# TensorE's units beside attention cut into parts of at most four products, shared results kept in a place of their own, the feed-forward's first stages eight slots earlier

## The chip, the core and the metric

The program runs on one core of one Trainium2 chip. A core has five engines with a queue each: TensorE (PE, matrix products into PSUM banks), VectorE (DVE), ScalarE (ACT), GpSimd (POOL) and SyncE (SP, which only issues DMAs here). The metric is the device time of one execution in microseconds (us), the median over several runs.

## What is computed

One layer: an attention of an unusual kind, then a feed-forward part with routed experts, each between layer norms and with a residual. The input x is 4 batches of 2048 rows of 256 numbers, all in fp32. The reference, cut to what matters:

```python
# attention: per head one scalar z for each key and query row
Z = concat([k @ Wproj.T, q @ Wproj.T], axis=1)
# out_i = sum_j max(0, 1 - |z_i - z_j| / b_h) * v_j   (the reference sorts and sums prefixes)
ctx = ctx / T
x = x + layernorm(attention(layernorm(x)))
# feed-forward on h = layernorm(x), 8192 rows
gu = h @ shared_gate_up_w                       # 256 -> 2 x 512
shared = silu(gu[:, :512]) * gu[:, 512:] @ shared_down_w
shared = shared * sigmoid(h @ shared_gate_w)
w, idx = top_k(softmax(h @ gate_w), 8)          # 64 experts, capacity 128 each
y = routed experts on the gathered rows, weighted and added
x = x + layernorm(y + shared)
```

## The kernel before

**The attention loop.** The kernel doesn't sort. For each of the 4 batches b it goes through 256 slots (`SLOTS`), 1024 tiles in all. A tile is the 128x2048 matrix of weights of 128 keys of one head against all 2048 queries. In slot n, ScalarE writes |z_query - z_key| for a tile (line 1085), VectorE turns it into min(., 1) - 1 in place (line 1406), and TensorE multiplies it with V in `tensor_step` (line 886): four matmul calls of 128x32 by 512 columns, on four groups of array columns side by side. Step n takes quarter c of tile n - c, so that a tile is fully used three steps after its own. The tiles lie in a ring of 8 (`NTB`), and ScalarE waits with tile n until tile n - 8 is used (`tile_used`), which means until TensorE has begun step n - 5. 64 slots (a quad) finish four heads. In the first slots of the next quad TensorE transposes their results (`tensor_quad_out`, line 847) and VectorE copies them (lines 1323 and 1331).

**Own tiles.** ScalarE needs longer for a tile than VectorE, so VectorE makes some tiles alone (lines 1428 and 1404). `own_tiles` picks them: it adds up, slot by slot, what VectorE has left after the work beside attention, with the costs in `WEIGHTS`, and gives it a tile when it is far enough ahead. It picks 86 tiles, 19, 23, 22 and 22 in the four batches.

**The work beside attention.** All else that the loop carries is written in `timetable(b)`: one list of (slot, unit) for each of TensorE, VectorE, ScalarE and SyncE. Each engine's program goes through the slots in order and, ahead of the tile of slot n, does the entries that are due. The lists fix only the order on each engine. When an entry really runs is set by semaphores. In batch 0 the loop carries the front of batches 1 to 3 (f): for each chunk k of 512 rows load, norm, transposes (`xT`), values (`v`), then the sixteen steps `z` that build z for the batch, with weights that SyncE loads into a ring of three buffers (`ml`). In batches 1 to 3 it carries the rest of batch b - 1: the residual and its norm (rows, `rows_at`), then from `rest_at(k)`, for each chunk k: norm (`hn`), transposes (`hT`), router logits (`lg`), routing on VectorE and GpSimd (`rm`, `re`, `sc`, `sm`), the transposed mask (`mT`), the shared gate and up products (`gu`: 4 pieces m, each one unit for gate and one for up), and the shared down products (`dn`), whose results go to y_rows in DRAM.

**Units on TensorE.** `tensor_stage` issues a whole unit at once, ahead of the step of its slot. A unit ends in one PSUM bank; banks 4, 5 and 6 are used in turn (`bank_uses`). In matmul calls: `gu` 2 of 512 columns, `z` 2 of 512 in each of 16 entries, `v` 4 of 256, `lg` 8 of 65 in two entries, `dn` 8 of 256, `hT`, `xT` and `mT` 4 transposes. The profile shows two MATMUL instructions for a call (line 828: 512 instructions for 256 calls), and one for a transpose.

**The place of the shared results.** `y_of(b, k)` shares its place in `scr` with `h_of(b, k)`. So `dn` on VectorE waits for the store of h, and `hn` of chunk k waits for the store of y of chunk k - 1 (line 1224).

**After the loop.** The last batch's rest runs in a tail: its routing, then 64 expert steps (`tensor_tail`), with the shared units of chunks 1 to 3, one in every second step (`shared_in_step`), and a last pass over all rows.

## Time and profile before

| | |
|---|---|
| median of 3 runs | 2416.1 us (2409.9 to 2416.64) |
| the profiled execution | 2415.98 us |
| its span, first to last instruction | 2414.7 us |
| VectorE, ScalarE, TensorE busy | 83%, 81%, 80% |
| mean granted clock of TensorE | 0.919 |
| ScalarE's first tile of the loop starts at | 80.18 us |
| the four batches of the loop begin on VectorE at | 83, 594, 1064 and 1536 us |
| the loop ends, the tail begins | 2003 us |
| expert steps, last pass | 2097 to 2330 us, 2330 us to the end |

An engine's busy share is a mean over stages with different limits. Within the loop three engines are busy most of the time and hand tiles on to each other, so what counts is which of them waits, and for whom.

### The profile page before, as it was taken

To read this page: it belongs to the slowest core of one execution; us is meant where nothing else is said; L and a number is where in the kernel's file an instruction comes from. 1 tells how busy PE (TensorE), PEld (TensorE's weight loads), DVE (VectorE), ACT (ScalarE), POOL (GpSimd) and SP (SyncE) were. 2 spreads that over 40 slices of the span, in tenths; PEclk is the share of its full clock that TensorE was granted. 3 is DMA by queue.
4 is the path that set the end of the run, shared out by engine and by line. 5 is a ranking of instruction groups with operands and counts; after the bars stand their busy time and mean duration, and the time that the engine had idled before them with its cause. 6 is when DMAs were issued, how large, how long until landed. Compare 5 with 4: busy or idle time off the path is not lost.

```text
span 2414.7 us, 30201 instructions
## 1 busy us (share of the span) xinstructions
PE 1930.5 (80%) x11666; PEld 760.1 (31%) x11666; DVE 1994.5 (83%) x2847; ACT 1948.2 (81%) x1290; POOL 1007.4 (42%) x372
## 2 busy tenths in 40 slices
PE   7689889789668889886798898777898896899920
PEld 4333233233112223221132232212223224677710
DVE  4598888887999998999998999998989897644348
ACT  2498998898999999999998999999999995122223
POOL 1010110100336367263383574550853764377754
PEclk9899999899889999998998999988999998898965
DMA  6326244335120212131202021312020306488779
GB/s 224 133 66 222 81 154 149 110 127 185 57 105 12 90 31 81 42 114 44 96 20 92 20 94 33 116 38 96 27 85 20 101 3 148 125 227 228 182 207 306
DMA packets 182037, 259.23 MB, mean 107 GB/s; under 512 B 22280, under 2 KB 162184, under 8 KB 173704
## 3 DMA queue, kind: packets, MB, share of 16 engines
q1 hardware_dynamic: 167408, 237.83, 29.3%
q0 software_dynamic: 12288, 18.88, 4.1%
q8 instruction: 93, 1.52, 0.3%
q10 hardware_dynamic: 2200, 0.60, 0.1%
q14 instruction: 48, 0.39, 0.0%
HBM read 187.25 MB, written 70.03 MB: 107 GB/s over the span
## 4 chain that ended last, share of the span: by engine, by line
PE 32%; DVE 26%; ACT 26%; POOL 6%; issue 5%; DMA 3%; SPq 0%; DVEq 0%; POOLq 0%; ACTq 0%
ACT TB L1085 25%; PE ps L886 12%; DVE TB L1406 10%; PE ps L790 5%; DVE TB L1428 4%; PE ps L828 4%; PE ps L835 3%; DVE st L1139 3%; DVE TB L1404 2%; PE ps L981 2%; POOL scr L1579 2%; POOL rs L1561 2%; POOL ve L1559 2%; DMA y_rows<-ZB 1%; PE ps L773 1%
## 5 line engine op out<-in xcount | busy, mean ns | idle before, releaser
L1085 ACT ACTIVATE TB<-ZB,nzk 128x2048 f32<-128x2048 f32 x938 | 1795.6, 1997 | 144.2 <-PE ps L886 98.0
L886 PE MATMUL ps<-TB,V 128*32 128x512 f32 x8192 | 1098.1, 636 | 282.5 <-DVE TB L1406 266.0
L1406 DVE TENSOR_SCALAR TB<-TB 128x2048 f32<-128x2048 f32 x938 | 1130.0, 1230 | 100.0 <-ACT TB L1085 97.9
L886 PEld LDWEIGHTS ps<-TB,V 128*32 128x32 f32 x8192 | 206.7, 112 | 1004.7 <-DVE TB L1406 630.7
L1579 POOL TENSOR_TENSOR scr<-ebase,scr 128x256 f32<-128x256 f32 x12 | 510.5, 42542 | 0.0
L1559 POOL TENSOR_SCALAR ve<-mv 128x4 f32<-128x4 f32 x56 | 82.5, 1472 | 800.4 <-DVE mv L1143 800.4
L828 PE MATMUL ps<-XF,wsgu 128*128 128x512 f32 x512 | 259.8, 632 | 1.2 <-DVE TB L1313 0.7
L1428 DVE SCALAR_TENSOR_TENSOR TB<-ZB,kz 128x2048 f32<-128x2048 f32 x86 | 212.4, 2469 | 4.2 <-PE ps L886 4.2
L1577 POOL TENSOR_TENSOR scr<-ebase,scr 128x4 f32<-128x4 f32 x12 | 28.5, 2378 | 390.0 <-DVE scr L1267 390.0
L1118 ACT ACTIVATE ZB<-ps 128x128 f32<-128x128 f32 x64 | 17.8, 278 | 184.0 <-PE ps L981 155.8
L828 PEld LDWEIGHTS ps<-XF,wsgu 128*128 128x128 f32 x512 | 91.8, 197 | 148.6 <-issue 141.6
L1404 DVE TENSOR_SCALAR TB<-TB,kz 128x2048 f32<-128x2048 f32 x86 | 121.6, 1414 | 0.0
L1684 POOL DMA_INDIRECT y_rows<-ZB x64 | 102.2, 1597 | 31.4 <-issue 14.9
L1561 POOL TENSOR_TENSOR rs<-ve,mhalf 128x4 f32<-128x4 f32 x56 | 106.1, 1894 | 4.7
L790 PE MATMUL ps<-scr,XF 128*128 128x512 f32 x192 | 100.1, 644 | 0.0
L835 PE MATMUL ps<-wsdn,XF 128*128 128x256 f32 x384 | 89.3, 386 | 0.0
L1670 POOL DMA_INDIRECT TB<-h_rows,ZB x64 | 63.5, 993 | 60.0 <-ACT ZB L1125 25.8
L1526 DVE COPY ZB<-ps 128x256 f32<-128x256 f32 x64 | 27.0, 422 | 67.0 <-PE ps L971 54.2
L835 PEld LDWEIGHTS ps<-wsdn,XF 128*128 128x128 f32 x384 | 71.0, 190 | 28.8 <-issue 20.1
L1610 POOL TENSOR_TENSOR scr<-scr,ctxn 128x1024 f32<-128x1024 f32 x12 | 61.0, 5080 | 36.0 <-DVE ctxn L1149 36.0
L847 PE MATMUL ps<-ident,cT 128*128 128x128 f32 x248 | 41.9, 295 | 39.3 <-DVE ctxn L1331 39.0
L1323 DVE COPY cT<-ps 128x512 f32<-128x512 f32 x60 | 41.3, 688 | 37.3 <-PE ps L886 37.2
(190 smaller groups left out, 1621.8 us busy)
## 6 DMA issues: line engine op xcount, KB each, us to landing
ZB<-zq_rows SPq DMA_DIRECT2D x64, 1024.0 KB, 7.0
scr<-fused_w SPq DMA_DIRECT2D x48, 512.0 KB, 3.5
TB<-in_egu_w SPq DMA_DIRECT2D x44, 256.0 KB
y_rows<-zero SPq DMA_DIRECT2D x20, 512.0 KB, 4.8
fused_w<-TB SPq DMA_DIRECT2D x4, 2048.0 KB, 13.7
TB<-y_rows SPq DMA_DIRECT2D x16, 512.0 KB, 8.5
XF<-in_x SPq DMA_DIRECT2D x24, 256.0 KB, 3.2
v_rows<-scr SPq DMA_DIRECT2D x24, 256.0 KB, 2.1
```

Source lines behind the costliest of these rows:

```text
L790: ins = pe.matmul(ps[bank][:, :], view(X0, NT * c + tt, [[16, 128]]), w[:, c, :], start=(tt == 0 and c == 0), stop=(tt == 15 and c == 1))
L828: ins = pe.matmul(ps[bank][:, :], wsgu[:, c, o:o + 128], hT_of(b, k)[:, c, :], start=(c == 0), stop=(c == 1))
L835: ins = pe.matmul(ps[bank][:, 256 * t:256 * t + 256], act_of(b)[:, mm, 128 * (2 * i + t):128 * (2 * i + t) + 128], wsdn[:, mm, :], start=( ...
L886: ins = pe.matmul(ps[c][32 * j:32 * j + 32, :], V[:, o:o + 32], tile(t)[:, 512 * c:512 * c + 512], start=(kb == 0), stop=(kb == KB - 1))
L1085: act.activation(tile(e), zrow(head), ACT.Abs, bias=nzk[b][:, kb * H + g:kb * H + g + 1], scale=1.0).then_inc(s_abs, 1)
L1404: dve.tensor_scalar(T, T, top, top, ALU.min, ALU.subtract).then_inc(s_bump, 1)
L1406: dve.tensor_scalar(T, T, 1.0, 1.0, ALU.min, ALU.subtract).then_inc(s_bump, 1)
L1428: dve.scalar_tensor_tensor(tile(e), zrow(head), kz[:, 0, kb * H + g:kb * H + g + 1], zrow(head), ALU.subtract, ALU.max, reverse0=True).the ...
L1559: pool.tensor_scalar(ve[s][:, :], view(mv[s][:, 0, 1:2], 0, [[2, 4]]), eps, None, ALU.add).then_inc(s_p, 1)
L1561: pool.tensor_tensor(rs[s][:, :], ve[s][:, :], mhalf[:, 0:4], ALU.pow).then_inc(done, 1)
L1579: pool.tensor_tensor(E4[:, :, 0:64], view(ebase[:, 0:1], 0, [[0, 4], [0, 64]]), E4[:, :, 0:64], ALU.pow).then_inc(s_ex, 1)
L1684: pool.indirect_dma_start(Y[c], bass.IndirectOffsetOnAxis(ap=idx2[:, order[n]:order[n] + 1].bitcast(u32), axis=0), ye[n % NX], None, compu ...
```

## The change

Every entry of TensorE's list is now a unit and a part of it (`PARTS`): `gu` in 2 parts of one matmul call, `z` in 32 of one call, `v` in 2 and `lg` in 4 parts of two calls. `dn` becomes 4 units of 128 rows in place of 2 of 256, each in 2 parts of two calls. The largest part is so four MATMUL instructions. The timetable gives each part a slot of its own: `gu` takes two slots of every three, `dn` the eight slots from r + 46 to r + 53, `z` eight slots of every nine, 36 in place of 32 for a batch. Rows stand 10 slots apart in place of 12 and begin one slot earlier, `rest_at` is 52 + 48k in place of 60 + 48k, the front's chunks stand 9 apart in place of 10. Within the rest most of VectorE's entries stand one to four slots later after `rest_at` than before.

In batches 0 to 2 the results of `dn` go to `wv_sb` and a free part of `scr` (`y_rows`), stored by two DMAs of 256 KB each in place of one of 512 KB. `dn` no longer waits for the store of h but for the store of the y before it, and `hn` of chunk k waits for the store of h of chunk k - 1 and for its transposes in place of the store of y. In the tail the 30 shared units become 36, spread over steps 1 to 59.

```diff
-           "rm": 15, "re": 8, "sc": 14, "sm": 5, "sg": 4, "gu": 7, "dn": 8}
+           "rm": 15, "re": 8, "sc": 14, "sm": 5, "sg": 4, "gu": 7, "dn": 4}
+
+PARTS = {"xT": 1, "hT": 1, "mT": 1, "zT": 1, "v": 2, "z": 32, "lg": 4, "gu": 2, "dn": 2}
...
-    return 8 + 12 * blk
+    return 7 + 10 * blk
...
-    return 60 + 48 * blk
+    return 52 + 48 * blk
...
-    return 2 + 86 * (f - 1) + 10 * blk
+    return 1 + 85 * (f - 1) + 9 * blk
...
-    return front_at(f, 3) + 20 + 2 * tt
+    return front_at(f, 3) + 21 + 9 * tt // 4
...
-            sy += [(r - 2, "xl", p, k), (r + 9, "h", p, k), (r + 31, "cum", p, k), (r + 58, "w2", p, k), (r + 50, "y", p, k)]
+            sy += [(r - 2, "xl", p, k), (r + 9, "h", p, k), (r + 33, "cum", p, k), (r + 58, "w2", p, k), (r + 58, "y", p, k)]
             dv += [(r, "xst", p, k, 0), (r + 1, "xst", p, k, 1), (r + 5, "hn", p, k, 0), (r + 6, "hn", p, k, 1),
-                   (r + 12, "hT", p, k), (r + 20, "lg", p, k), (r + 21, "rm", p, k), (r + 23, "re", p, k),
-                   (r + 28, "sc", p, k), (r + 40, "sg", p, k), (r + 54, "sm", p, k)]
+                   (r + 12, "hT", p, k), (r + 21, "lg", p, k), (r + 22, "rm", p, k), (r + 24, "re", p, k),
+                   (r + 31, "sc", p, k), (r + 41, "sg", p, k), (r + 55, "sm", p, k)]
             ac += [(r + 15, "hT", p, k)]
-            pe += [(r + 8, "hT", p, k, 0), (r + 9, "hT", p, k, 1), (r + 15, "lg", p, k, 0), (r + 16, "lg", p, k, 1),
-                   (r + 24, "mT", p, k)]
+            pe += [(r + 8, ("hT", p, k, 0)), (r + 9, ("hT", p, k, 1)), (r + 27, ("mT", p, k))]
+            pe += [(r + 15 + t, ("lg", p, k), t) for t in range(4)]
             for m in range(4):
-                for up in range(2):
-                    pe += [(r + 17 + 6 * m + 3 * up, "gu", p, k, m, up)]
-                ac += [(r + 23 + 6 * m, "gu", p, k, m)]
-                dv += [(r + 24 + 6 * m, "gu", p, k, m)]
-            for i in range(2):
-                pe += [(r + 42 + 3 * i, "dn", p, k, i)]
-                dv += [(r + 46 + 3 * i, "dn", p, k, i)]
+                g = r + 19 + 6 * m
+                pe += [(g + 3 * up + c, ("gu", p, k, m, up), c) for up in range(2) for c in range(2)]
+                ac += [(g + 7, "gu", p, k, m)]
+                dv += [(g + 7, "gu", p, k, m)]
+            for i in range(4):
+                pe += [(r + 46 + 2 * i + h, ("dn", p, k, i), h) for h in range(2)]
+                dv += [(r + 50 + 2 * i, "dn", p, k, i)]
...
-            dv += [(r - 1, "fst", f, k, 0), (r, "fst", f, k, 1), (r + 3, "fn", f, k, 0), (r + 4, "fn", f, k, 1), (r + 9, "xT", f, k, 0), (r + 9, "xT", f, k, 1)]
-            pe += [(r + 5, "xT", f, k, 0), (r + 6, "xT", f, k, 1)]
+            dv += [(r, "fst", f, k, 0), (r + 1, "fst", f, k, 1), (r + 5, "fn", f, k, 0), (r + 6, "fn", f, k, 1),
+                   (r + 12, "xT", f, k, 0), (r + 12, "xT", f, k, 1)]
+            pe += [(r + 8, ("xT", f, k, 0)), (r + 9, ("xT", f, k, 1))]
             for i in range(2):
-                pe += [(r + 10 + 2 * i, "v", f, k, i)]
-                dv += [(r + 14 + 2 * i, "v", f, k, i)]
-                sy += [(r + 15 + 2 * i, "vs", f, k, i)]
+                pe += [(r + 13 + 2 * i + t, ("v", f, k, i), t) for t in range(2)]
+                dv += [(r + 18 + 2 * i, "v", f, k, i)]
+                sy += [(r + 19 + 2 * i, "vs", f, k, i)]
         for tt in range(16):
-            pe += [(z_at(f, tt), "z", f, tt)]
+            pe += [(z_at(f, tt) + c, ("z", f), 2 * tt + c) for c in range(2)]
             sy += [(z_at(f, tt) - 5, "ml", f, tt)]
         r = z_at(f, 15)
-        dv += [(r + 6, "z", f), (r + 13, "zT", f)]
-        pe += [(r + 7, "zT", f)]
-        sy += [(r + 14, "zq", f)]
+        dv += [(r + 5, "z", f), (r + 10, "zT", f)]
+        pe += [(r + 6, ("zT", f))]
...
+        o += gate_units(b, k) + [("dn", b, k, i) for i in range(4)]
...
-    return o[n // 2:n // 2 + 1] if n >= 0 and n % 2 == 0 else []
+    return [u for i, u in enumerate(o) if 1 + 60 * i // len(o) == n]
...
+            if b == last:
+                return rows4(view(T0, 1024 * k, [[256, 4], [1, 256]]))
+            return [wv_sb[:, 0, :], wv_sb[:, 1, :], view(S0, 3652, [[1, 256]]), view(S0, 3908, [[1, 256]])]
...
+                    sp.wait_ge(q_h[3], 16 * b)
...
-                kk, m = use["dn", b, k, 1]
+                kk, m = use["dn", b, k, 3]
                 sp.wait_ge(empty[kk], m + 1)
-                sp.dma_start(Yv[0][4 * b + k], y_of(b, k)).then_inc(q_y, 16)
+                for i in range(2):
+                    src = view(y_rows(b, k)[2 * i], 0, [[256, 2], [1, 256]])
+                    sp.dma_start(Yv[0][4 * b + k][:, 2 * i:2 * i + 2, :], src).then_inc(q_y, 16)
...
+        def tensor_stage(unit, part=None):
+            for p in range(PARTS[unit[0]]) if part is None else (part,):
+                tensor_part(unit, p)
+
...
+            out_, ends = ps[bank], p == PARTS[what] - 1
+            if p == 0 and m:
...
+                if p == 0:
+                    for kk, mm in [use["xT", b, j, h] for j in range(4) for h in range(2)]:
...
+                if b and c == 0:
...
-                for c in range(2):
-                    ins = pe.matmul(ps[bank][:, :], view(X0, NT * c + tt, [[16, 128]]), w[:, c, :],
-                                    start=(tt == 0 and c == 0), stop=(tt == 15 and c == 1))
-                if tt == 15:
+                ins = pe.matmul(out_[:, :], view(X0, NT * c + tt, [[16, 128]]), w[:, c, :], start=(p == 0), stop=ends)
+                if ends:
                     ins.then_inc(full[bank], 1)
-                elif b:
+                elif b and c:
                     ins.then_inc(s_zm, 1)
...
+                if p == 0:
+                    for c in range(2):
+                        kk, mm = use["hT", b, k, c]
+                        pe.wait_ge(empty[kk], mm + 1)
+                o = NS * unit[4] + 128 * i
+                ins = pe.matmul(out_[:, :], wsgu[:, p, o:o + 128], hT_of(b, k)[:, p, :], start=(p == 0), stop=ends)
+                if ends:
+                    ins.then_inc(full[bank], 1)
...
+                if p == 0:
+                    kk, mm = use["gu", b, k, 3, 1]
...
+                for mm in (2 * p, 2 * p + 1):
+                    ins = pe.matmul(out_[:, 0:256], act_of(b)[:, mm, 128 * i:128 * i + 128], wsdn[:, mm, :],
+                                    start=(mm == 0), stop=(mm == 3))
+                if ends:
+                    ins.then_inc(full[bank], 1)
...
-                    dve.wait_ge(q_y, 16 * (4 * b + k))
+                    dve.wait_ge(q_h[k - 1], 16 * (b + 1))
+                    kk, mm = use["hT", b, k - 1, 1]
+                    dve.wait_ge(full[kk], mm + 1)
...
-                    dve.wait_ge(q_y, 192)
+                    dve.wait_ge(q_h[3], 16 * last)
...
-                    dve.wait_ge(q_h[k], 16 * (b + 1))
+                    dve.wait_ge(q_y, 32 * (4 * b + k))
...
-                for t in range(2):
-                    ti = 2 * i + t
-                    ins = dve.tensor_scalar(y_of(b, k)[:, ti, :], ps[bank][:, 256 * t:256 * t + 256],
-                                            sg[:, 4 * k + ti:4 * k + ti + 1], None, ALU.mult)
-                ins.then_inc(empty[bank], 1)
+                dve.tensor_scalar(y_rows(b, k)[i], ps[bank][:, 0:256], sg[:, 4 * k + i:4 * k + i + 1], None,
+                                  ALU.mult).then_inc(empty[bank], 1)
```

## Rows read from the trace of the kernel before

**Rows 1.** The page: granted clock by slices, the two costliest groups.

```profile
PEclk9899999899889999998998999988999998898965
...
L1085 ACT ACTIVATE TB<-ZB,nzk 128x2048 f32<-128x2048 f32 x938 | 1795.6, 1997 | 144.2 <-PE ps L886 98.0 <-DMA ZB<-zq_rows 45.8
...
L1406 DVE TENSOR_SCALAR TB<-TB 128x2048 f32<-128x2048 f32 x938 | 1130.0, 1230 | 100.0 <-ACT TB L1085 97.9
```

**Rows 2.** Busy time by windows, batches 0 and 2 (us, busy with instruction counts, clock).

```profile
83.00:594.00 511.00, 434.54 (x2570) 159.71 (x2570) 426.20 (x507) 460.58 (x240) 48.18 (x24) 0.93 0.40 139
...
1064.00:1536.00 472.00, 390.78 (x2480) 119.48 (x2480) 435.29 (x534) 453.96 (x255) 240.53 (x37) 0.94 0.19 66
```

**Rows 3.** ScalarE's tiles by lines: windows 83:594, 594:1064, 1064:1536, 1536:2003.

```profile
L1085 ACT ACTIVATE TB<-ZB,nzk 128x2048 f32<-128x2048 f32 x240 | 461.1, 1994 | 50.9 <-PE ps L886 45.9 <-DMA ZB<-zq_rows 4.8
...
L1085 ACT ACTIVATE TB<-ZB,nzk 128x2048 f32<-128x2048 f32 x232 | 444.0, 1998 | 19.4 <-PE ps L886 19.2
...
L1085 ACT ACTIVATE TB<-ZB,nzk 128x2048 f32<-128x2048 f32 x235 | 449.3, 1998 | 18.0 <-PE ps L886 18.0
...
L1085 ACT ACTIVATE TB<-ZB,nzk 128x2048 f32<-128x2048 f32 x233 | 445.2, 1997 | 14.9 <-PE ps L886 14.9
```

**Rows 4.** TensorE in order of time, in the `z` stage of batch 1.

```profile
246.74 2.09 PE L790 MATMUL ps<-scr,XF 128*128 128x512 f32 x4
248.76 1.92 PE L886 MATMUL ps<-TB,V 128*32 128x512 f32 x16
250.61 2.09 PE L790 MATMUL ps<-scr,XF 128*128 128x512 f32 x4
```

**Rows 5.** ScalarE's tiles, the three `z` stages: windows 197:255, 357:416, 529:594.

```profile
L1085 ACT ACTIVATE TB<-ZB,nzk 128x2048 f32<-128x2048 f32 x25 | 49.0, 1998 | 10.2 <-PE ps L886 6.8 <-DMA ZB<-zq_rows 3.4
...
L1085 ACT ACTIVATE TB<-ZB,nzk 128x2048 f32<-128x2048 f32 x28 | 54.3, 1995 | 7.1 <-PE ps L886 7.1
...
L1085 ACT ACTIVATE TB<-ZB,nzk 128x2048 f32<-128x2048 f32 x30 | 58.5, 1997 | 7.4 <-PE ps L886 7.4
```

**Rows 6.** VectorE in order of time, the end of batch 0.

```profile
591.17 0.42 DVE L1185 COPY scr<-ps 128x256 f32<-128x256 f32 x1 [3.51 <-PE ps L790]
```

**Rows 7.** ScalarE's tiles, slots 0 to 58: windows 594:706, 1064:1175, 1536:1647.

```profile
L1085 ACT ACTIVATE TB<-ZB,nzk 128x2048 f32<-128x2048 f32 x53 | 101.4, 1993 | 13.0 <-PE ps L886 13.0
...
L1085 ACT ACTIVATE TB<-ZB,nzk 128x2048 f32<-128x2048 f32 x57 | 108.6, 1990 | 4.8 <-PE ps L886 4.8
...
L1085 ACT ACTIVATE TB<-ZB,nzk 128x2048 f32<-128x2048 f32 x57 | 108.5, 1989 | 5.1 <-PE ps L886 5.1
```

**Rows 8.** TensorE in order of time, `gu` and `dn` units of batch 2.

```profile
1405.99 1.98 PE L828 MATMUL ps<-XF,wsgu 128*128 128x512 f32 x4
1407.91 2.78 PE L886 MATMUL ps<-TB,V 128*32 128x512 f32 x24
1410.62 1.98 PE L828 MATMUL ps<-XF,wsgu 128*128 128x512 f32 x4
...
1431.64 3.72 PE L835 MATMUL ps<-wsdn,XF 128*128 128x256 f32 x16
1435.29 2.78 PE L886 MATMUL ps<-TB,V 128*32 128x512 f32 x24
1438.00 3.72 PE L835 MATMUL ps<-wsdn,XF 128*128 128x256 f32 x16
```

**Rows 9.** ScalarE in order of time, behind a `dn` pair of batch 1.

```profile
966.30 5.79 ACT L1085 ACTIVATE TB<-ZB,nzk 128x2048 f32<-128x2048 f32 x3 [1.40 <-PE ps L886]
972.66 3.90 ACT L1085 ACTIVATE TB<-ZB,nzk 128x2048 f32<-128x2048 f32 x2 [0.57 <-PE ps L886]
```

**Rows 10.** A window of batch 2, then ScalarE's longest wait beside it.

```profile
1285.00:1299.00 14.00, 13.48 (x48) 5.54 (x52) 7.92 (x8) 9.41 (x5) 0.00 (x0) 0.51 0.76 300
...
1299.82 3.90 ACT L1085 ACTIVATE TB<-ZB,nzk 128x2048 f32<-128x2048 f32 x2 [2.76 <-PE ps L886]
```

**Rows 11.** The chain that ended last, shares by line, the expert steps.

```profile
by line: PE ps L981 17.4%; issue 13.1%; DMA y_rows<-ZB 12.9%; PE ps L828 12.7%; PE ps L990 7.5%; PE ps L835 6.1%; PE ps L939 5.6%; PE ps L971 4.3%; POOL y_rows L1684 4.0%; POOL TB L1670 3.6%; DMA TB<-y_rows 2.2%; PE ps L940 1.9%; DMA TB<-h_
```

More of the change, by code:

```diff
@@ L148, in bank_uses @@
         for e in timetable(b)[0]:
-            if e[1] == "z" and e[3] or e[1] == "lg" and e[4]:
-                continue
-            take({"z": e[1:3], "lg": e[1:4]}.get(e[1], e[1:]), 4 + ring % 3)
-            ring += 1
+            if e[2:] in ((), (0,)):
+                take(e[1], 4 + ring % 3)
+                ring += 1
     for t in range(4):
@@ L623, in sync_stage @@
                 elif k:
-                    sp.wait_ge(q_y, 64 * b)
+                    sp.wait_ge(q_h[3], 16 * b)
+                    kk, mm = use["hT", b - 1, 3, 1]
+                    sp.wait_ge(full[kk], mm + 1)
                 else:
@@ L752, in flip, with tensor_part @@
             ins.then_inc(full[k], 1)
-        def tensor_stage(what, b, k=0, i=0, up=0):
-            unit = {"gu": (what, b, k, i, up), "zT": (what, b), "lg": (what, b, k), "mT": (what, b, k),
-                    "z": (what, b)}.get(what, (what, b, k, i))
+        def tensor_stage(unit, part=None):
+            for p in range(PARTS[unit[0]]) if part is None else (part,):
+                tensor_part(unit, p)
+        def tensor_part(unit, p):
+            what, b = unit[:2]
+            k, i = (unit[2:] + (0, 0))[:2]
             bank, m = use[unit]
-            if m and (what != "z" or k == 0) and (what != "lg" or i == 0):
+            out_, ends = ps[bank], p == PARTS[what] - 1
+            if p == 0 and m:
                 pe.wait_ge(empty[bank], m)
@@ L805, in tensor_stage @@
             elif what == "lg":
-                for c in range(2):
-                    kk, mm = use["hT", b, k, c]
-                    pe.wait_ge(empty[kk], mm + 1)
-                pe.wait_ge(q_ffw, 48)
-                for t in (2 * i, 2 * i + 1):
-                    for c in range(2):
-                        ins = pe.matmul(ps[bank][:, 65 * t:65 * t + 65], hT_of(b, k)[:, c, 128 * t:128 * t + 128], wg_sb[:, c, :],
-                                        start=(c == 0), stop=(c == 1))
-                if i:
+                if p == 0:
+                    for c in range(2):
+                        kk, mm = use["hT", b, k, c]
+                        pe.wait_ge(empty[kk], mm + 1)
+                    pe.wait_ge(q_ffw, 48)
+                for c in range(2):
+                    ins = pe.matmul(out_[:, 65 * p:65 * p + 65], hT_of(b, k)[:, c, 128 * p:128 * p + 128], wg_sb[:, c, :],
+                                    start=(c == 0), stop=(c == 1))
+                if ends:
                     ins.then_inc(full[bank], 1)
@@ L898, in tensor_program @@
                     tensor_bias()
-                elif unit[0] == "z":
-                    for tt in range(16):
-                        tensor_stage("z", 0, tt)
                 else:
-                    tensor_stage(*unit)
+                    tensor_stage(unit)
             for b in range(NB):
@@ L945, in tensor_tail @@
             for unit, _ in tail_first():
-                tensor_stage(*unit)
-                if unit[0] == "lg":
-                    tensor_stage(*unit, 1)
+                tensor_stage(unit)
             k, m = use["pv",]
@@ L953, in tensor_tail @@
             pe.matmul(ps[7][:, 0:32], shift, CS[:, :, 127], start=True, stop=True).then_inc(full[7], 1)
-            tensor_stage("dn", last, 0, 0)
+            for i in range(2):
+                tensor_stage(("dn", last, 0, i))
             tensor_slots(0, 0)
             tensor_slots(0, 1)
-            tensor_stage("dn", last, 0, 1)
+            for i in range(2, 4):
+                tensor_stage(("dn", last, 0, i))
             for n in range(-1, NE + 1):
@@ L963, in tensor_tail @@
                 for unit in shared_in_step(n):
-                    tensor_stage(*unit)
+                    tensor_stage(unit)
                 if n + 1 < NE:
@@ L1031, in scalar_stage @@
                 if k and m == 0:
-                    kk, mm = use["dn", b, k - 1, 1]
+                    kk, mm = use["dn", b, k - 1, 3]
                     act.wait_ge(full[kk], mm + 1)
                 elif m == 0 and b != last:
-                    kk, mm = use[("dn", b - 1, 3, 1) if b else ("z", last)]
+                    kk, mm = use[("dn", b - 1, 3, 3) if b else ("z", last)]
                     act.wait_ge(full[kk], mm + 1)
@@ L1502, in vector_tail @@
                 vector_slots(0, i, v)
-            for i in range(2):
+            for i in range(4):
                 vector_stage(v, "dn", b, 0, i)
```

68 lines of the change are left out of this document (29 added, 39 removed).

## Prediction

> **What bounds the kernel now.** I read the page first, then the idle time of ScalarE by windows, then the order of time where it is idle. The loop is a chain of three engines and a ring of eight tiles. ScalarE's 938 tiles take 1795.6 us and it is idle for 144.2 us before them, 98.0 us for TensorE and 45.8 us for the loads of z [rows 1]. Of this some 41 us lie before its first tile at 80.18 us. In the four windows of the loop it is idle for 50.9, 19.4, 18.0 and 14.9 us, together 103.2 us [rows 3]. All else on ScalarE is fixed work, so these 103 us are all that the change can win in the loop; the number of tiles that VectorE takes over could also move it. VectorE has little room: it is busy for 435.29 us of 472 in batch 2, TensorE for 390.78 [rows 2]. TensorE is no bound by its sum, but ScalarE waits for step n - 5, so a TensorE that lags some five microseconds stops it.
>
> The 103 us are of three kinds. In the three `z` stages 10.2, 7.1 and 7.4 us, 24.7 together [rows 5]. In slots 0 to 58 of batches 1 to 3, where TensorE has hardly anything but tiles, 13.0, 4.8 and 5.1 us [rows 7]; there it is VectorE that is late, with rows, copies and own tiles. What is left of batches 1 to 3, where the rest's units stand, is 52.3 - 22.9 = 29.4 us. What is left of batch 0 is 50.9 - 24.7 = 26.2 us.
>
> **Part by part.** *Splitting `z`.* In the order of time the `z` call pair comes every 250.61 - 246.74 = 3.87 us, and two steps stand between [rows 4]. A step alone takes 0.86 us: (2.78 - 1.92) of x24 against x16 [rows 4, 8]. So a pair costs 3.87 - 1.72 = 2.15 us. Its four MATMULs of 512 columns need 4 x 0.43 = 1.72 us, as half a step does for four side by side; the other 0.43 us is the way into the unit and out again. TensorE never waits there: two slots take 3.87 us, while ScalarE wants 1.91 us a tile (449.3 / 235) and skips own tiles [rows 3]. 32 slots take 61.9 us, ScalarE with 28, 27 and 28 tiles wants 53.5, 51.6 and 53.5, 27.1 us less in all, and 24.7 us of idle time is what is read [rows 5]: nine tenths. In the new table 36 slots hold 32 parts, each with a way in and out of its own. That is 36 x 0.86 + 32 x (0.86 + 0.43) = 72.2 us. I worked the sum of `own_tiles` through with the new tables: 86 tiles again, 20, 22, 22, 22, and 5, 5 and 6 of them in the `z` stages. ScalarE wants 59.2, 59.2 and 57.3 us, 40.9 us less than TensorE takes; nine tenths of it are 37. So the `z` stages cost 37 - 25 = **+12 us**. From below the cost is -25 us (the way in and out is hidden, TensorE needs 36 x 0.86 + 32 x 0.86 = 58.5 us and ScalarE never waits), from above +16 us (nothing absorbed). I take +12 since the pair's period shows the way in and out unhidden.
>
> The Trainium skill (TensorE: Matmul & The Clock Gate, section "Step-by-step: what each phase is for") says that TensorE's queue pulls weight loads ahead of running matmuls, so that the next weights load while the present ones stream. By that rule a part would cost its columns alone and the `z` stages would win 25 us in place of losing 12. The trace agrees within a step, where four small loads hide, and not at the change of unit.
>
> *Splitting `gu`, `dn`, `v`, `lg`.* A `gu` unit costs (1410.62 - 1405.99) - 3 x 0.86 = 2.05 us, 1.72 of columns and 0.33 of way; a `dn` unit (1438.00 - 1431.64) - 2.58 = 3.78 us [rows 8]. After: a `gu` part 1.19, a `dn` part 16 / 4 MATMULs, 0.86 + 0.33 = 1.19. A batch gets 32 more visits from `gu` and 24 more from `dn`, 56 x 0.33 = 18.5 us of TensorE, some 21 with `lg`. It lies in the 472 - 391 = 81 us that TensorE isn't busy [rows 2], and costs nothing as long as that cover holds: in the `gu` slots three slots need 2.58 + 2.38 = 4.96 us against 3 x 1.91 = 5.73, or 5.2 where an own tile falls. In the eight `dn` slots it needs 8 x 2.05 = 16.4 us against 15.3, a lag of 1 to 2 us, where today one unit puts 3.78 us ahead of one step and the pair ends in waits of 1.40 and 0.57 us [rows 9]. Batches 1 to 3 have twelve such pairs, and not all of them end in a wait.
>
> The other large waits have units of four to eight MATMULs falling on the quad's transposes while the granted clock is low: 0.51 in 14 us of batch 2, the lower of the two levels, 1.2 GHz, with 2.76 us as the longest wait [rows 10]. Before it fell TensorE had waited for VectorE. Moved by eight slots, the routing of chunk 1 no longer stands at slots 128 to 134, and no slot gets more than one part. The clock itself will go on falling. Bounds for the busy part: 29.4 us won if every wait goes, 0 if the lag only comes back as waits for VectorE. I take six tenths, **-18 us**: by ScalarE's order of time the waits behind `dn` are some 12 us of it and the collisions some 12, estimates both.
>
> *Batch 0 outside `z`.* The `v` units become halves, chunks stand closer, and the norm stands one slot later behind GpSimd. The bound is 0 to -26 us; the first 10 are the start-up, which waits for the load of x, as before. I take **-6 us**. *The end of batch 0.* VectorE waits 3.51 us for the last `z` products [rows 6] and ScalarE then pays in slots 5 to 8 of batch 1, the reason for 13.0 us where the others have 5 [rows 7]. The last part now stands two slots earlier, which is 2 x (1.91 - 0.86) = 2 us, and the own tile of slot 4 is gone: **-3 us** (0 to -8).
>
> *The place of y, the waits of `hn` and `dn`, two stores for one, rows 10 apart.* The old waits don't show in VectorE's idle time, so taking them away wins nothing by itself: 0. VectorE's `dn` now waits for the y store of 40 slots before, some 75 us: 0. One entry bears watching: the store of h of chunk 0 now stands at slot 61 on SyncE's queue, ahead of the first load of z for the next quad. It waits for VectorE's norm of slot 58, and the loads behind it with it, and those ScalarE needs at slot 66. VectorE is a slot or three behind ScalarE, so I put it at 0, and at +3 us a batch if it isn't. *More rows for slots 7 to 50:* VectorE's work there is the same in fewer slots, and fewer own tiles are put there: 0, at most +4 us.
>
> *The tail.* `dn` is 6.1% of the chain of the expert steps [rows 11], 14 us of 233. The same columns come in more visits at other steps: 0, between -4 and +4.
>
> **Sum.** +12 - 18 - 6 - 3 = -15 us. The profiled execution is 2415.98 us, within 0.2 us of the median 2416.1, so I forecast **2401 us**.
>
> **Rivals.**
> *A, the forecast* (0.45): the `z` stages lose, the rest wins more. 2401, its own range 2390 to 2412.
> *B, the way in and out is hidden* (0.17): the weight loads of a single call are prefetched, the `z` stages lose their 25 us and the rest stays as said: 2416 - 25 - 27 = 2364 us. For it: a step's loads are hidden; against it: the 0.43 us in every pair of the `z` stage.
> *C, nothing in sum* (0.18): VectorE is the true second bound, its room of 37 us in 472 [rows 2] is scattered, and waits for TensorE come back as waits for VectorE; the `z` loss and the batch 0 gain cancel: 2416 us, 2411 to 2421.
> *D, slower* (0.20): TensorE's ways in and out. The `z` stages cost the full +16, and the split units fill the slots so far that what batches 1 to 3 win is eaten by lag in the `gu` and `dn` slots: 2416 + 16 - 4 = 2428 us. It decides as soon as the other terms bring less than 12 to 16 us; the 72.2 us for slots that ScalarE wants in 59 speak for it, the 81 us of room in the other batches against it.
>
> **Numbers.** The range goes from 2374 (between A and B, leaving most of B out) to 2428. A change within 0.3% is 2408.9 to 2423.3, about what a measurement here can't tell from none. Faster: most of A and all of B, 0.60. Same: C and the upper end of A, 0.19. Slower: 0.21.
>
> **What would show it.** `z` stages of 70 to 73 us each, single `z` parts 2.15 us apart from each other with a step between, and 10 to 15 us of ScalarE's idle time in each: A or D. Parts 1.7 us apart: B. In batches 1 to 3, idle time before ScalarE's tiles falls from 52.3 us to some 30, and no wait follows `dn`: A; stays above 45: C or D. TensorE busy about 410 us a batch in place of 391. The prediction is wrong above all if VectorE's lateness in slots 0 to 58 grows with the closer rows, or if a load of z is late at slot 66.

## The result, and the profile after

The changed kernel takes **2403.03 us** (median of 5 runs, 2395.99 to 2404.75) against 2416.1; the ratio is 0.9944, 95% interval 0.9927 to 0.996, so it is faster by 0.4 to 0.7%. Its profiled execution is 2404.75 us (span 2403.4), 11.2 us under that of before, where 2401 was forecast.

The page, granted clock by slices and the group of ScalarE's tiles:

```profile
PEclk9899999999889999998898999989999998898965
...
L1100 ACT ACTIVATE TB<-ZB,nzk 128x2048 f32<-128x2048 f32 x938 | 1798.5, 1994 | 129.7 <-PE ps L902 80.3
```

ScalarE has the same 938 tiles and is idle before them for 129.7 us in place of 144.2 [rows 1]. By the four windows of the loop (batches 0 to 3, 82:594, 594:1063, 1063:1531 and 1531:1992, as [rows 3]):

```profile
L1100 ACT ACTIVATE TB<-ZB,nzk 128x2048 f32<-128x2048 f32 x239 | 461.1, 1993 | 52.2 <-PE ps L902 46.0 <-DMA ZB<-zq_rows 5.9
...
L1100 ACT ACTIVATE TB<-ZB,nzk 128x2048 f32<-128x2048 f32 x232 | 445.3, 1995 | 15.8 <-PE ps L902 14.7
...
L1100 ACT ACTIVATE TB<-ZB,nzk 128x2048 f32<-128x2048 f32 x235 | 449.5, 1992 | 12.6 <-PE ps L902 12.1
...
L1100 ACT ACTIVATE TB<-ZB,nzk 128x2048 f32<-128x2048 f32 x234 | 446.7, 1996 | 7.8 <-PE ps L902 7.5
```

Together 88.4 us in place of 103.2: 14.8 us won. The tiles' own busy time gives 3 back (1795.6 to 1798.5 us), which leaves the loop some 11 us shorter. The three `z` stages (windows 183:256, 350:416, 529:594) answer to [rows 5]:

```profile
L1100 ACT ACTIVATE TB<-ZB,nzk 128x2048 f32<-128x2048 f32 x31 | 60.7, 1996 | 15.3 <-PE ps L902 10.8 <-DMA ZB<-zq_rows 4.5
...
L1100 ACT ACTIVATE TB<-ZB,nzk 128x2048 f32<-128x2048 f32 x30 | 58.6, 1998 | 9.1 <-PE ps L902 9.1
...
L1100 ACT ACTIVATE TB<-ZB,nzk 128x2048 f32<-128x2048 f32 x29 | 57.3, 1999 | 10.5 <-PE ps L902 10.4
```

34.9 us in place of 24.7: **10.2 lost**. These windows leave out the ends of some stages, before and after. Counted over whole stages, from TensorE's first `z` product to its last (windows 182:260, 352:424 and 518:594 after, 191:258, 358:420 and 530:594 before), it is 15.6, 9.6 and 10.5 us in place of 10.4, 7.1 and 7.4: 35.7 for 24.9, 10.8 lost. Slots 0 to 58 of batches 1 to 3 (windows 594:704, 1063:1176, 1531:1642) answer to [rows 7]:

```profile
L1100 ACT ACTIVATE TB<-ZB,nzk 128x2048 f32<-128x2048 f32 x55 | 104.9, 1990 | 7.4 <-PE ps L902 7.4
...
L1100 ACT ACTIVATE TB<-ZB,nzk 128x2048 f32<-128x2048 f32 x58 | 110.3, 1988 | 4.9 <-PE ps L902 4.9
...
L1100 ACT ACTIVATE TB<-ZB,nzk 128x2048 f32<-128x2048 f32 x57 | 108.4, 1990 | 5.5 <-PE ps L902 5.5
```

17.8 us in place of 22.9, and all of the difference in the first batch. Batch 0 outside `z` has 52.2 - 34.9 = 17.3 in place of 26.2, and the busy part of batches 1 to 3 has 36.2 - 17.8 = 18.4 in place of 29.4.

TensorE in order of time, a `z` stage (as [rows 4]), then `gu` and `dn` parts of batch 2 (as [rows 8]):

```profile
243.72 1.06 PE L902 MATMUL ps<-TB,V 128*32 128x512 f32 x8
244.71 1.23 PE L806 MATMUL ps<-scr,XF 128*128 128x512 f32 x2
245.88 1.06 PE L902 MATMUL ps<-TB,V 128*32 128x512 f32 x8
246.87 1.23 PE L806 MATMUL ps<-scr,XF 128*128 128x512 f32 x2
...
1405.50 1.92 PE L902 MATMUL ps<-TB,V 128*32 128x512 f32 x16
1407.36 1.12 PE L843 MATMUL ps<-XF,wsgu 128*128 128x512 f32 x2
...
1435.97 1.06 PE L902 MATMUL ps<-TB,V 128*32 128x512 f32 x8
1436.96 1.13 PE L851 MATMUL ps<-wsdn,XF 128*128 128x256 f32 x4
1438.03 1.07 PE L902 MATMUL ps<-TB,V 128*32 128x512 f32 x8
```

(x8 is one step, x2 and x4 are one part.) A slot with a `z` part takes 246.87 - 244.71 = 2.16 us, one with a `dn` part 2.06, so a visit, as this document calls a part or unit between two steps, is 1.30 and 1.20 us beside the step's 0.86. Busy time by windows for batches 0 and 2 (columns as in [rows 2]):

```profile
83.00:594.00 511.00, 447.19 (x2570) 142.46 (x2570) 428.80 (x508) 459.28 (x239) 40.01 (x24) 0.97 0.41 139
...
1063.00:1531.00 468.00, 402.67 (x2484) 111.52 (x2480) 434.30 (x534) 455.42 (x255) 236.96 (x36) 0.94 0.20 66
```

### The profile page after: what moved, and what is told of

It reads as the page before. It is cut to its first block, busy times and chain, and to the rows that moved or that the text cites. A ratio compares the mean times of both kernels' runs of the same rounds, so it can differ in the third digit from the quotient of the medians.

```text
span 2403.4 us, 30276 instructions
## 1 busy us (share of the span) xinstructions
PE 1969.0 (82%) x11666; PEld 716.3 (30%) x11666; DVE 1993.8 (83%) x2847; ACT 1951.5 (81%) x1290; POOL 992.5 (41%) x372
## 4 chain that ended last, share of the span: by engine, by line
PE 36%; ACT 29%; DVE 22%; POOL 5%; issue 5%; DMA 3%; SPq 0%; DVEq 0%; POOLq 0%; ACTq 0%
ACT TB L1100 28%; PE ps L902 14%; DVE TB L1420 8%; PE ps L806 6%; PE ps L843 4%; DVE TB L1442 4%; PE ps L851 3%; DVE st L1154 2%; PE ps L994 2%; POOL scr L1593 2%; PE ps L790 1%; POOL rs L1575 1%; POOL ve L1573 1%; DVE TB L1418 1%; PE ps L952 1%
## 5 line engine op out<-in xcount | busy, mean ns | idle before, releaser
L1100 ACT ACTIVATE TB<-ZB,nzk 128x2048 f32<-128x2048 f32 x938 | 1798.5, 1994 | 129.7 <-PE ps L902 80.3
L902 PE MATMUL ps<-TB,V 128*32 128x512 f32 x8192 | 1114.1, 631 | 229.4 <-DVE TB L1420 218.8
L902 PEld LDWEIGHTS ps<-TB,V 128*32 128x32 f32 x8192 | 189.8, 111 | 899.0 <-DVE TB L1420 540.4
L1573 POOL TENSOR_SCALAR ve<-mv 128x4 f32<-128x4 f32 x56 | 68.5, 1223 | 779.4 <-DVE mv L1158 779.4
L843 PE MATMUL ps<-XF,wsgu 128*128 128x512 f32 x512 | 282.7, 646 | 3.4 <-DVE TB L1318 3.4
L1591 POOL TENSOR_TENSOR scr<-ebase,scr 128x4 f32<-128x4 f32 x12 | 35.1, 2921 | 348.7 <-DVE scr L1284 348.7
L843 PEld LDWEIGHTS ps<-XF,wsgu 128*128 128x128 f32 x512 | 83.0, 194 | 179.1 <-issue 171.7
L806 PE MATMUL ps<-scr,XF 128*128 128x512 f32 x192 | 117.9, 696 | 0.0
L851 PE MATMUL ps<-wsdn,XF 128*128 128x256 f32 x384 | 108.6, 406 | 0.0
L1575 POOL TENSOR_TENSOR rs<-ve,mhalf 128x4 f32<-128x4 f32 x56 | 96.2, 1718 | 4.7
L806 PEld LDWEIGHTS ps<-scr,XF 128*128 128x128 f32 x192 | 49.4, 304 | 78.0 <-issue 78.0
```

The lines of the kernel that those rows point to most:

```text
L806: ins = pe.matmul(out_[:, :], view(X0, NT * c + tt, [[16, 128]]), w[:, c, :], start=(p == 0), stop=ends)
L843: ins = pe.matmul(out_[:, :], wsgu[:, p, o:o + 128], hT_of(b, k)[:, p, :], start=(p == 0), stop=ends)
L851: ins = pe.matmul(out_[:, 0:256], act_of(b)[:, mm, 128 * i:128 * i + 128], wsdn[:, mm, :], start=(mm == 0), stop=(mm == 3))
L902: ins = pe.matmul(ps[c][32 * j:32 * j + 32, :], V[:, o:o + 32], tile(t)[:, 512 * c:512 * c + 512], start=(kb == 0), stop=(kb == KB - 1))
L1100: act.activation(tile(e), zrow(head), ACT.Abs, bias=nzk[b][:, kb * H + g:kb * H + g + 1], scale=1.0).then_inc(s_abs, 1)
L1573: pool.tensor_scalar(ve[s][:, :], view(mv[s][:, 0, 1:2], 0, [[2, 4]]), eps, None, ALU.add).then_inc(s_p, 1)
```

## The experiments

Each idle time below is ScalarE's before its tiles. The kernel before had a median of 2411.62 us in the first group (first four runs), 2416.73 in the second (next four), 2412.68 in the third and 2414.1 in the last; ratios are against it, so they compare across groups better than times do. The change itself was not run again in any group; its ratio of 0.9944 is from its own measurement.

**1. `z` in pairs, two slots apart.**

```diff
-pe += [(z_at(f, tt) + c, ("z", f), 2 * tt + c) for c in range(2)]
+pe += [(z_at(f, tt), ("z", f), 2 * tt + c) for c in range(2)]
```

> The changed kernel with both calls of a z step issued in one slot again, at the new spacing of nine slots for four steps (visits of TensorE to z halved, columns the same). Theory W (each visit to a z unit costs 0.43 us that nothing hides, and the z stages are bound by TensorE): 36 slots need 36 x 0.86 + 16 x 2.15 = 65.4 us in place of 72.2, ScalarE's idle time in the z stages falls by some 16 us, time 2387 us (2383 to 2392). Rival V (VectorE is the second bound and takes over as soon as TensorE is faster): no gain, 2401 to 2404 us.

Measured: 2381.84 us, ratio 0.9875 (0.9854 to 0.9897), 0.7% below the change. TensorE in its `z` stage:

```profile
242.49 2.09 PE L806 MATMUL ps<-scr,XF 128*128 128x512 f32 x4
244.51 1.92 PE L902 MATMUL ps<-TB,V 128*32 128x512 f32 x16
246.37 2.09 PE L806 MATMUL ps<-scr,XF 128*128 128x512 f32 x4
```

A pair is 246.37 - 242.49 = 3.88 us with two steps, 2.16 without; two single parts are 2 x 1.30 = 2.60. Batch 0's idle time falls from 52.2 us to

```profile
L1100 ACT ACTIVATE TB<-ZB,nzk 128x2048 f32<-128x2048 f32 x239 | 457.9, 1992 | 38.4 <-PE ps L902 34.7 <-DMA ZB<-zq_rows 3.4
```

So W holds and V does not. Over whole stages the idle time in `z` falls from 35.7 to 22.9 us, 12.8 in place of the 16 expected; the time lies just below the stated 2383 to 2392. In the profiled executions another 9 us of its gain lie in batches 1 to 3 (26.9 in place of 36.2), where the edit changes no order; there the run had 27 us at the low clock in slots 60 to 255, the change's own 51. Why is not shown.

**2. The kernel before, with `z` in single products.** The line of its timetable; the rest of the edit (not shown) only lets one call stand as an entry:

```diff
-pe += [(z_at(f, tt), "z", f, tt)]
+pe += [(z_at(f, tt) + c, "z", f, tt, c) for c in range(2)]
```

> The kernel before with only one edit: the two calls of a z step stand in two slots following each other, so that each of the 32 slots of a z stage has one call. Theory W: 32 slots need 32 x (0.86 + 1.29) = 68.8 us in place of 61.9, three times, so the time rises by some 19 us to 2435 us (2430 to 2438). Rival H (the way into a unit is hidden when it holds a single call): 2413 to 2418 us, no change.

Measured: 2439.72 us, ratio 1.0106 (1.0084 to 1.0129), 26 us slower by the ratio, a little more than the 2430 to 2438 expected. Batch 0's idle time goes from 50.9 [rows 3] to 68.7, 17.8 us more, of which 12.7 lie in the three whole `z` stages (37.6 in place of 24.9); batches 1 to 3 stay within 2 us of before. Some 7 us of the profiled span lie behind the loop, where the edit touches nothing; I have no cause for them. So some 18 us, and not all 26, are shown to be the price of the visits.

```profile
L1085 ACT ACTIVATE TB<-ZB,nzk 128x2048 f32<-128x2048 f32 x240 | 465.0, 1994 | 68.7 <-PE ps L886 59.5 <-DMA ZB<-zq_rows 8.8
```

**3. Both parts of `gu` and `dn` units in one slot.**

```diff
-pe += [(g + 3 * up + c, ("gu", p, k, m, up), c) for up in range(2) for c in range(2)]
+pe += [(g + 3 * up, ("gu", p, k, m, up), c) for up in range(2) for c in range(2)]
...
-pe += [(r + 46 + 2 * i + h, ("dn", p, k, i), h) for h in range(2)]
+pe += [(r + 46 + 2 * i, ("dn", p, k, i), h) for h in range(2)]
```

> The changed kernel with the two parts of each gu unit and of each dn unit (of four calls) issued together in the slot of the first part; all slots else unchanged. Theory P (the cut into parts is what removes ScalarE's waits in batches 1 to 3): half of what they won comes back, 2409 to 2412 us. Theory M (the earlier slots, the distance from the quad's transposes and the spread of dn over eight slots win it, the cut of gu and dn into parts is worth nothing): 2400 to 2405 us, with TensorE busy for some 13 us less a batch.

Measured: 2416.51 us, ratio 1.0011 (0.9997 to 1.0024): the whole gain of the change is gone. Batches 1 to 3 have 22.9, 11.5 and 15.7 us of idle time, 13.9 more than the change. In slots 60 to 255 it is 14.3, 6.6 and 10.1, together 31.0, where the kernel before had 29.4 and the change has 18.4. So theory M falls, and P with it in size: all comes back, not half. The earlier slots and the `dn` units of half the rows, which this kernel keeps, win nothing there without the cut into parts.

**4. The kernel before, with only the new place of y, its waits and its two stores.** Cut to the main lines:

```diff
+return [wv_sb[:, 0, :], wv_sb[:, 1, :], view(S0, 3652, [[1, 256]]), view(S0, 3908, [[1, 256]])]
...
-dve.wait_ge(q_y, 16 * (4 * b + k))
+dve.wait_ge(q_h[k - 1], 16 * (b + 1))
...
-dve.wait_ge(q_h[k], 16 * (b + 1))
+dve.wait_ge(q_y, 32 * (4 * b + k))
```

> The kernel before with only the place of the shared results changed (wv_sb and a free part of scr, two stores, the new waits of hn, dn and load a); timetable and units as before. As forecast the old waits cost nothing: 2413 to 2419 us, no change. Rival Y (the waits for the y store did hold VectorE back): 3 us or more faster.

Measured: 2416.95 us, ratio 1.0014 (0.9999 to 1.0029). No gain, as forecast; rival Y falls.

**5. `z` in fours, four slots apart.**

```diff
-pe += [(z_at(f, tt) + c, ("z", f), 2 * tt + c) for c in range(2)]
+pe += [(z_at(f, tt - tt % 2), ("z", f), 2 * tt + c) for c in range(2)]
```

> The changed kernel with the calls of two z steps (four calls) issued in one slot, every 4.5 slots. Theory W (each visit costs 0.43 us): 36 slots need 36 x 0.86 + 8 x 3.87 = 62 us in place of 65.4 with pairs, some 8 us less idle time than with pairs, time about 0.9845 of the kernel before (pairs: 0.9875). Rival L (a single visit of 3.9 us holds up the steps, or two loads of weights of 3.4 us each no longer fit into 4.5 slots of 1.9 us): as pairs or slower, 0.987 or above.

Measured: **2376.18 us**, ratio 0.9826 (0.9813 to 0.984), the best of all. Rival L falls.

```profile
241.56 3.64 PE L902 MATMUL ps<-TB,V 128*32 128x512 f32 x32
245.13 3.81 PE L806 MATMUL ps<-scr,XF 128*128 128x512 f32 x8
248.87 3.64 PE L902 MATMUL ps<-TB,V 128*32 128x512 f32 x32
```

Four products and four steps take 248.87 - 241.56 = 7.31 us, and 7.31 - 4 x 0.86 = 3.87 = 4 x 0.86 + 0.43. So a visit costs 0.43 us beside its columns, be they those of one, two or four products. Four products in a row make TensorE late by 3.87 us, and no more idle time comes of it: over whole `z` stages it is 18.5 us, against 22.9 with pairs and 35.7 with single calls, so the look-ahead of five tiles takes the delay up. By the ratios fours are 12 us faster than pairs, by the medians 6; in the profiled executions they have 66.9 us of idle time in the loop against 65.3. So the step from single calls to pairs is clear of all noise, and the size of the one from pairs to fours is not.

Where the fixed time goes can be read from the loads of weights (PEld), here of the change and then of the fours:

```profile
244.71 0.51 PEld L806 LDWEIGHTS ps<-scr,XF 128*128 128x128 f32 x2 [0.84 <-issue]
245.87 0.16 PEld L902 LDWEIGHTS ps<-TB,V 128*32 128x32 f32 x8 [0.65 <-issue]
...
245.13 3.09 PEld L806 LDWEIGHTS ps<-scr,XF 128*128 128x128 f32 x8 [0.84 <-issue]
```

The first load of a visit begins at 244.71, with the visit itself. The unit that loads weights has been idle for 0.84 us by then, and the step's last products began at 244.19, so their 0.43 us of columns are through before the load starts. The same holds for the first load of the next step, at 245.87. Within a visit of eight MATMULs all eight loads are done in 3.09 us, beside the running products. So what is paid is the way in and the way out, once each.

**6 and 7. Only `dn`, only `gu` whole** (one of the two lines of experiment 3 each).

> The changed kernel with the two parts of a dn unit together (2.05 us of TensorE in every second slot, none in the other). The run with gu and dn whole gave 1.0011 of the kernel before, the changed kernel 0.9944. If the loss is shared evenly: 0.9975. If it is all gu's: 0.9944. If it is all dn's: 1.001.

> The changed kernel with the two parts of a gu unit together (2.05 us of TensorE in one slot of three). If the loss of the run with both whole is shared evenly: 0.9975 of the kernel before. If it is all gu's: 1.001. If all dn's: 0.9944.

Measured: `dn` whole 2403.98 us, 0.9944 (0.9931 to 0.9958), no different from the change; `gu` whole 2406.48 us, 0.9958 (0.9945 to 0.9972), some 3 us more, not told apart from none. One by one they cost 0 and 3 us and together 16 by the ratios, 12 by the profiled executions of experiment 3 and the change. The extra lies in batches 1 and 3 of experiment 3, with 41 and 24 us at the low clock, where the change has 24 and 3. That is a correlation; why it isn't a sum stays open.

With `dn` whole, though its time is that of the change, the waits behind `dn` are back, here in batches 1, 2 and 3:

```profile
962.66 19.05 ACT L1100 ACTIVATE TB<-ZB,nzk 128x2048 f32<-128x2048 f32 x10 [1.62 <-PE ps L902]
...
1430.05 19.04 ACT L1100 ACTIVATE TB<-ZB,nzk 128x2048 f32<-128x2048 f32 x10 [1.62 <-PE ps L902]
...
1891.70 19.05 ACT L1100 ACTIVATE TB<-ZB,nzk 128x2048 f32<-128x2048 f32 x10 [1.61 <-PE ps L902]
```

Summed over batches 1 to 3, ScalarE's waits for one of the five steps behind a `dn` part or unit are 11.1 us before, 3.6 in the change and 10.3 here. The total is no larger (36.9 us against 36.2) since other waits are missing, above all the 4.6 us in batch 2 that the change has at a low clock (below).

**8. The rest four slots later.**

```diff
-    return 52 + 48 * blk
+    return 56 + 48 * blk
```

> The changed kernel with rest_at at 56 + 48k in place of 52 + 48k, all else the same. Theory S (what wins is the distance of chunk 1's routing and first products from the quad's transposes at slots 128 to 134, so the earlier start counts): 3 to 6 us slower, 0.9960 to 0.997 of the kernel before. Theory P (the cut into parts wins, the place hardly matters): 0.993 to 0.9955, as the changed kernel.

Measured: 2405.62 us, 0.995 (0.9936 to 0.9963), inside the range of P and below that of S. By the ratios these four slots are worth 1 or 2 us, and by the intervals, which overlap, not more than some 7, though chunk 1's transposed mask and first `gu` parts now stand at slots 123 to 133 again, beside the quad's transposes.

**9 to 12. Filling TensorE.** In batches 1 to 3, each of the 70 slots from slot 52 on that carry no part gets a product whose result is used by nothing (the output's computation is unchanged).

```diff
+def tensor_filler(q):
+    k, m = use["qt", q - 1, 3]
+    pe.wait_ge(empty[k], m + 1)
+    pe.matmul(ps[k][:, 0:512], ident[:, :], wsgu[:, 0, 0:512], start=True, stop=True)
...
+if b and n >= 52 and 8 <= n % 64 < 63 and not due:
+    tensor_filler(q)
```

> The changed kernel with one useless matmul call (128x128 by 512 columns, into the bank of the quad's transposes once that is free) in each of the slots from 52 on of batches 1 to 3 that hold no part, some 70 a batch. The profiles so far: in slots 60 to 255 of a batch ScalarE is idle for 1 us where TensorE's clock is never low, 2.3 us at 3.4 us of low clock, 8 us at 24 us. Theory C (what is left of ScalarE's idle time in the busy part is made by stretches of low clock, and these begin where TensorE had little to do, as in the slots between dn of one chunk and lg of the next): the low stretches in slots 100 to 160 go, the idle time of the busy parts falls from 18.4 us to 5 or less, time 0.989 to 0.991 of the kernel before. Rival F (the clock falls whatever stands in the free slots, and 70 x 1.2 us more of TensorE only makes it late): 0.996 or above.

The same on `z` in fours, and with the 44 free slots below slot 52 as well:

> The same fill on top of z in fours (0.9826 without it). Theory C: 0.977 to 0.980. Rival F: 0.984 or above.

> z in fours, and the fill also in the free slots below 52 of batches 1 to 3, where TensorE has little beside tiles. There VectorE is late and not TensorE, so by theory C the clock will rise there but the time stays that of the run with the fill from slot 52 on, within 2 us; if the fill makes TensorE late behind VectorE's bursts, 3 to 8 us slower.

Measured: 2524.46 us, ratio 1.0455 (1.0436 to 1.0475); 2496.61, 1.0349 (1.0328 to 1.0369); 2524.89, 1.0461 (1.0441 to 1.048). The low clock is gone from slots 60 to 255, as theory C had it, but the time, for which C had a gain, is by the ratios 123, 126 and 153 us worse than without the fill. The range of rival F (0.996 or above) holds, but not its reason, that the clock falls all the same. The fill below slot 52 was expected to cost 8 us at most and cost 27. TensorE in order of time in experiment 9:

```profile
810.14 1.06 PE L907 MATMUL ps<-TB,V 128*32 128x512 f32 x8
811.14 1.12 PE L870 MATMUL ps<-wsgu,ident 128*128 128x512 f32 x2
812.20 1.06 PE L907 MATMUL ps<-TB,V 128*32 128x512 f32 x8
```

A filled slot takes 2.06 us and ScalarE's tile 1.91: TensorE is the bound. So the last run halves the columns.

> The changed kernel, plus in each of the 70 slots of batches 1 to 3 (from slot 52 on) that carry no part a product of 256 columns whose result is used by nothing: half the columns of the earlier fill, so that such a slot costs TensorE 0.86 + 0.33 + 0.43 = 1.62 us and stays under ScalarE's 1.91, where the full fill took 2.05. Theory G (the stretches at the low clock are what costs in the busy part, and the full fill failed only because a slot became longer than ScalarE's tile): the low clock still disappears from slots 60 to 255, ScalarE's idle time there falls from 18.4 us (8.4, 7.7, 2.3) to 3 to 8, and the time is 2389 to 2396. Theory L (what costs is how little free time TensorE has to catch up after it is held up, by VectorE or a load, whatever the clock): the low clock may be gone, but the idle time of the busy part rises to 30 us or more, and the time is 2415 to 2440. A time of 2400 to 2410 would say that the two cancel: what the clock gives back is what the fill takes.

Measured: 2443.25 us, ratio 1.011 (1.0092 to 1.0129). Its order of time, its busy time by windows (slots 60 to 255 of batch 1, then the whole batch), ScalarE's tiles in batch 1, and the busy time of the change in the same slots:

```profile
809.34 1.06 PE L907 MATMUL ps<-TB,V 128*32 128x512 f32 x8
810.33 0.70 PE L870 MATMUL ps<-wsgu,ident 128*128 128x256 f32 x2
810.96 1.06 PE L907 MATMUL ps<-TB,V 128*32 128x512 f32 x8
...
703.00:1075.00 372.00, 361.53 (x2120) 109.58 (x2112) 332.47 (x404) 355.82 (x202) 199.57 (x22) 1.00 0.18 62
...
599.00:1075.00 476.00, 435.52 (x2594) 124.88 (x2594) 434.59 (x531) 452.51 (x253) 240.95 (x36) 0.97 0.18 59
...
L1108 ACT ACTIVATE TB<-ZB,nzk 128x2048 f32<-128x2048 f32 x232 | 445.2, 1993 | 23.5 <-PE ps L907 22.7
...
700.00:1063.00 363.00, 327.89 (x2000) 97.04 (x2000) 329.76 (x401) 354.58 (x201) 197.29 (x22) 0.97 0.19 63
```

The filled slot is now 1.62 us, under 1.91, no slot from 60 on is at the low clock, and the idle time of the busy part is 46.1 us (16.2, 15.4, 14.5) against 18.4. That is what theory L expected, with a time 3 us above its range. 70 x 0.63 = 44 us more work a batch make the batches 1 to 3 longer by 11.2 us each ((1431.7 - 1398.0) / 3, from the first tile of batch 1 to the loop's end), and 70 x 1.06 = 74 us make them longer by 38.1 ((1512.3 - 1398.0) / 3).

The stage's own rows explain the size. A slot with a `gu` or `dn` part takes 2.06 us, and ScalarE, which skips own tiles, asks for less than 1.91 a slot on the mean (445.2 us of tiles in 256 slots, 1.74). In slots 60 to 255 of the change TensorE is busy for 327.89 us of 363 in batch 1, 330.11 of 361 in batch 2 and 323.38 of 355 in batch 3 (windows 700:1063, 1170:1531, 1637:1992). That leaves 35, 31 and 32 us, 32.5 on the mean, and not the 65 of the whole batch. 44 us put into 32.5 are 11.5 too many, 74 are 41.5 too many, close to the 11.2 and 38.1 measured (an estimate from these rows). With the half fill TensorE is busy for 361.53 us and ScalarE for 355.82: TensorE is the bound again, at half the columns too. So neither fill tests theory G, and what the clock's return gives back was not measured.

## Why the prediction was right

The sum was -15 us, and ScalarE's idle time in the loop fell by 14.8; the time itself fell by 13.1 (medians) or 11.2 (profiled executions), the tiles' own busy time being 3 us longer. The signs of all terms and the mechanism of the `z` term were right. That the sum came within 2 us was in part luck: the largest term, the busy part, was 7 us too good, and the other three were together 7 us too bad (1.8, 2.9 and 2.6).

- **The `z` stages: +12 forecast, +10.2 measured (+10.8 over whole stages).** Parts stand 2.16 us apart. TensorE needs from the first part of the second stage to the end of the last 423.2 - 352.5 = 70.7 us, where 34 x 0.86 + 32 x 1.29 = 70.5. The third takes 71.9 us, both inside the 70 to 73 said; the first takes 76.6 (182.3 to 258.9), as before the change the first took 65.1 and the others 60.2. The idle times of the whole stages are 15.6, 9.6 and 10.5, two of them at the edges of the 10 to 15 said. Experiments 1, 2 and 5 show the cause: going to pairs gives back 17 us by the ratios and 12.8 of idle time in these stages, the opposite edit in the old kernel adds 17.8 us of idle time to batch 0, and four products a visit win 28 us by the ratios. Rival B (2364 us) is out. The Trainium skill's rule (TensorE: Matmul & The Clock Gate, section "Step-by-step: what each phase is for") that weight loads are pulled ahead of running matmuls would have made visits cost their columns alone. With one, two and four products a visit the traces show 0.43 us on top, and the first load of each visit begins only with the visit, so here it does not carry over a change of unit; the page binds it to conditions on row groups or the background weight buffer, and no run here shows which of them fails.
- **The busy part of batches 1 to 3: -18 forecast, -11.0 measured.** This term was over-sized, though within its bounds; the idle time of batches 1 to 3 is 36.2 us where some 30 were said. It rested on two estimates, 12 us of waits behind `dn` and 12 of collisions at a low clock; 18 of the 29.4 us were to go. The waits behind `dn` fall from 11.1 to 3.6 us. Behind most chunks none is left (batch 1, parts in slots 194 to 201, the tiles of slots 197 to 210, 14 without a gap, where [rows 9] had 1.40 and 0.57 us behind a pair):

```profile
953.26 27.49 ACT L1100 ACTIVATE TB<-ZB,nzk 128x2048 f32<-128x2048 f32 x14
```

 but the sign that was said, that no wait follows `dn`, did not come in full: chunk 3 of the same batch ends in waits of 0.74 and 2.11 us, at and behind a low clock. And with `dn` whole in the new kernel these waits are back while the time is the same, so they are not the gain by themselves. Undoing the `gu` and `dn` parts together brings 13.9 us of idle time back, so these splits do carry the term. The collisions at a low clock were to go, and they moved: window 1277:1291 of batch 2, TensorE in it and ScalarE beside it, as [rows 10].

```profile
1277.00:1291.00 14.00, 14.00 (x64) 4.76 (x64) 11.63 (x24) 9.34 (x6) 0.69 (x1) 0.62 0.00 0
...
1275.27 1.94 PE L902 MATMUL ps<-TB,V 128*32 128x512 f32 x8
1277.13 1.12 PE L827 MATMUL ps<-wg_sb,XF 128*128 128x65 f32 x4
1278.18 1.94 PE L902 MATMUL ps<-TB,V 128*32 128x512 f32 x8
...
1283.05 2.00 ACT L1100 ACTIVATE TB<-ZB,nzk 128x2048 f32<-128x2048 f32 x1 [2.72 <-PE ps L902]
1285.96 2.00 ACT L1100 ACTIVATE TB<-ZB,nzk 128x2048 f32<-128x2048 f32 x1 [0.91 <-PE ps L902]
1288.93 5.95 ACT L1100 ACTIVATE TB<-ZB,nzk 128x2048 f32<-128x2048 f32 x3 [0.97 <-PE ps L902]
```

 They no longer meet the quad's transposes; they meet the router logits (`lg`) and the first `gu` parts, which now stand there. A slot with an `lg` part takes 1278.18 - 1275.27 = 2.91 us at this clock, against 1.59 at the full one (815.17 - 813.58 in experiment 12) and ScalarE's 1.91. Before the clock fell TensorE had waited 2.33 us for VectorE, as before the change. Four slots later the units are no worse off (experiment 8). The closer rows and the `v` and `lg` parts were not undone by themselves.
- **Batch 0 outside `z`: -6 forecast, -8.9 measured. Its end: -3 forecast, -5.6 measured** (13.0 to 7.4 us in slots 0 to 58 of batch 1). No experiment takes these two apart; their causes are argued only. VectorE's wait for the last product fell from 3.51 [rows 6] to 2.23:

```profile
590.24 0.43 DVE L1200 COPY scr<-ps 128x256 f32<-128x256 f32 x1 [2.23 <-PE ps L806]
```

- **y, its waits and stores: 0 forecast, no gain measured**, by experiment 4 (1.0014, 0.9999 to 1.0029).
- **The extra visits: hidden.** TensorE's busy time in batch 2 is 402.67 us, not 410; its visits cost what was said (1.20 us a part), and why the sum is 7 us lower was not followed up. The cover is thinner than "81 us of room" had it: the units stand in slots 60 to 255, and there some 32 us a batch are left after the change, by experiment 12.
- **The tail: 0 forecast**; from the start of TensorE's last step in the loop (1993.8 us, before 2005.4) to the end of the span it is 409.6 us, before 409.3. Experiments 1, 3 and 5 to 8, with the tail of the change, have 409.1 to 413.2, so a difference of some 4 us would not be seen.
- **Rivals C and D** (2416 and 2428 us) are out as B is: the change is faster clear of noise, and batches 1 to 3 have 36.2 us of idle time, not above 45.
- **Risks that didn't come:** slots 0 to 58 of batches 2 and 3 stay at 4.9 and 5.5 us. None of the rows of batches 1 to 3 above names a load of z.
